# The output products of a pair-mixing kernel, taken image by image with a signal each

## The reference

```python
x = x + pair_mix(group_norm(x))     # layer 1
x = x + blur(group_norm(x))         # layer 2

# pair_mix, for v = group_norm(x) of shape (2, 64, 64, 64), last dimension D = 64
a = v @ Wa + ba
b = v @ Wb + bb
g = sigmoid(v @ Wg + bg)
ab = einsum('bijk,bikl->bijl', a, b)   # a 64x64 product per image and channel
return g * ab @ Wo + bo
```

## Time and profile before

| what | us |
|---|---|
| median of three runs | 68.85 |
| the runs | 68.38, 68.85, 69.01 |
| profiled execution, its time | 68.02 |
| profiled execution, its span | 66.2 |
| PE busy | 50.2 (76%) |
| DVE busy | 44.7 (67%) |
| POOL busy | 42.3 (64%) |
| ACT busy | 30.6 (46%) |

### The profile page before, as it was taken

How to read it: one execution, slowest core, us unless ns; L and a number is a source line. 1 busy time by engine, 2 the same in 40 slices (tenths; PEclk the granted TensorE clock), 3 DMA queues, 4 the chain that set the end, 5 groups by cost and what they waited for, 6 DMA issues and landing times.

```text
span 66.2 us, 2441 instructions
## 1 busy us (share of the span) xinstructions
PE 50.2 (76%) x1026; PEld 37.2 (56%) x1026; DVE 44.7 (67%) x123; ACT 30.6 (46%) x52; POOL 42.3 (64%) x52
## 2 busy tenths in 40 slices
PE   3999989876979979998629499867079659999100
PEld 3996967643749848676318178634069552464000
DVE  0092199989646598463999975499964399961750
ACT  5300012444554244956971963996621697423400
POOL 1000419469999999048999978486963719999300
PEclk9999999999999999999999999999995555558965
DMA  0799990000000000000000033100404000040074
GB/s 0 280 233 299 349 354 11 0 10 0 0 10 0 0 10 0 5 10 0 0 10 0 22 136 127 41 10 0 163 0 158 10 0 0 5 158 0 31 286 158
DMA packets 2603, 4.78 MB, mean 72 GB/s; under 512 B 288, under 2 KB 416, under 8 KB 2592
## 3 DMA queue, kind: packets, MB, share of 16 engines
q1 hardware_dynamic: 2592, 4.62, 19.7%
HBM read 2.52 MB, written 2.10 MB: 70 GB/s over the span
## 4 chain that ended last, share of the span: by engine, by line
PE 48%; DVE 26%; issue 6%; ACT 4%; DVEq 0%
PE ps_ag L665 10%; PE ps_ab L610 8%; PE ps_ot L650 7%; DVE x L441 5%; PE ps_ot L577 4%; PE ps_ab L634 4%; DVE zt L434 4%; DVE part L388 4%; PE ps_s L558 3%; DVE bsb L425 3%; PE ps_ag L598 3%; PE ps_ag L622 3%; DVE part L383 2%; PE ps_s L565 2%; ACT gate L305 2%
## 5 line engine op out<-in xcount | busy, mean ns | idle before, releaser
L242 POOL TENSOR_TENSOR y<-y,prod 128x512 f32<-128x512 f32 x12 | 16.5, 1379 | 3.8 <-DVE y L448 3.1
L208 POOL TENSOR_TENSOR rstd<-veps,half 128x2 f32<-128x2 f32 (+1 forms) x7 | 5.6, 802 | 12.6 <-DVE veps L418 12.4
L236 POOL TENSOR_TENSOR xb<-xs,par 128x512 f32<-128x512 f32 x8 | 10.5, 1338 | 1.5 <-issue 1.5
L327 ACT ACTIVATE prod<-x,coef 128x512 f32<-128x512 f32 x12 | 8.2, 712 | 4.4 <-POOL coef L219 4.4
L292 ACT ACTIVATE rt<-ps_ot 128x512 f32<-128x512 f32 x7 | 3.9, 595 | 11.3 <-PE ps_ot L577 11.3
L550 PE MATMUL ps_h<-zeros 128*128 128x128 f32 x46 | 8.2, 346 | 1.0 <-DVE zeros L457 1.0
L550 PEld LDWEIGHTS ps_h<-zeros 128*128 128x128 f32 x46 | 7.5, 252 | 1.0 <-DVE zeros L457 1.0
L448 DVE SCALAR_TENSOR_TENSOR y<-x,coef,y 128x512 f32<-128x512 f32 x6 | 6.7, 1118 | 1.9 <-POOL y L224 1.9
L298 ACT ACTIVATE at<-ps_ag,par 128x512 f32<-128x512 f32 x8 | 5.5, 687 | 5.0 <-PE ps_ag L598 4.8
L305 ACT ACTIVATE gate<-ps_ag,par 128x512 f32<-128x512 f32 x8 | 5.5, 682 | 4.1 <-PE ps_ag L622 4.1
L665 PE MATMUL ps_ag<-x,diag 128*128 128x512 f32 (+4 forms) x12 | 7.0, 719 | 0.0
(11 more groups left out here) (50 smaller groups left out, 80.4 us busy)
## 6 DMA issues: line engine op xcount, KB each, us to landing
xs<-x SPq DMA_DIRECT2D x8, 256.0 KB, 5.2
out<-y SPq DMA_DIRECT2D x8, 256.0 KB, 2.0
par<-params SPq DMA_DIRECT2D x1, 289.5 KB, 4.4
par<-params SPq DMA_DIRECT2D x1, 128.0 KB, 4.1
```

Of the source, the lines that this page charges most:

```text
L236: nc.gpsimd.tensor_tensor(xb[:, w, b, :, :], xs[:, w, b, :, :], bo.broadcast_to([128, ROWS, D]), ALU.add).then_inc(xb_ready, 1)
L242: return nc.gpsimd.tensor_tensor(y[:, w, b, :, :], y[:, w, b, :, :], prod[:, n % 2, k, :, :], ALU.add)
L327: nc.scalar.activation(prod[:, n % 2, k, :, :], x1[:, w, b, 1:ROWS + 1, k:D + k], ACT.Copy, scale=coef[:, w, b, k + 2:k + 3]).then_inc(pro ...
```

## The change

`product_o` goes over the images first: all sixteen products that write bank 0 of `ps_ot` (image 0), then the sixteen that write bank 1. `o_done` is raised at the end of each sixteen, so twice a wave, and each of the two x1_outs waits for its own signal. Which operands meet, and where each result lands, is the same as before.

```diff
             def x1_out(w, b):
-                if b == 0:
-                    dve.wait_ge(o_done, w + 1)
+                dve.wait_ge(o_done, 2 * w + b + 1)
                 dve.wait_ge(xb_ready, 2 * w + b + 1)
...
-                for r in range(ROWS):
-                    for h in range(2):
+                for b in range(2):
+                    for r in range(ROWS):
                         for t in range(2):
 
+                            h = b ^ t
                             last = nc.tensor.matmul(
-                                ps_ot[64 * t:64 * t + 64, h ^ t, 64 * r:64 * r + 64],
+                                ps_ot[64 * t:64 * t + 64, b, 64 * r:64 * r + 64],
                                 zt[64 * h:64 * h + 64, w, 128 * r + 64 * t:128 * r + 64 * t + 64],
                                 W_O[64 * h:64 * h + 64, :], start=True, stop=True)
-                last.then_inc(o_done, 1)
+                    last.then_inc(o_done, 1)
```

## The result

The changed kernel is slower: the ratio of its time to that of the kernel before is 1.0188 (95% interval 1.0153 to 1.0222) over 20 runs of each, about 1.3 us. The medians of all 20 are 69.53 and 69.07 us; they hold disturbed runs, which the ratio leaves out. The profiled execution took 69.10 us (68.02 before) with a span of 67.3 (66.2). Forecast were 70.6 us as the likeliest and 68.9 to 71.1 as the range.

What follows compares the result with a forecast made beforehand. The chain of waits was taken as the bound, through O at waves 0 and 3 only (TensorE busy 76%); 0.83 + 0.93 = 1.76 us on the 68.85 us median gave 70.6 us, range 68.9 to 71.1.

Steps and rivals of the forecast that it cites:

- Image 0's signal comes at the old end of the group: O group: image 0's sixteen products use two quadrants and need 16 rounds, as long as the whole group before.
- The even-pace rival: O group: two quadrants keep up, so the 0.61 us gain at wave 3 stands, 68.2 us; chance 0.07.
- Rounds of two last as long as rounds of four; k = 14: O group: a round starts two instructions, not four, in equal time; k, rounds added to the 16, taken as 14.
- Wave 0: +0.83 us: Wave 0's O at full clock: 14 x 0.059 us, all on the chain through product_g and the gate.
- Waves 1 and 2: nothing: O ends 0.83 us later but still before x1_out, which starts behind filter_right; zero cost.
- Wave 3: +0.93 us: Wave 3 at half clock: image 1's signal 1.54 us later, 0.61 us of it under the first x1_out.
- k from 9 to 16: The forecast's own span of added O rounds: 0.91 us (69.8) to 2.09 us (70.9), chance 0.58.
- the rival with k = 7: Case of far look-ahead (chance 0.27 for k 1 to 8): seven rounds added to O, 0.57 us, 69.4 us.
- The tail keeps its lengths: After wave 3's x1_outs: apart from their 0.9 us gap, the rest of the tail takes as long as before.
- Far look-ahead: O group: image 1 fills idle quadrants early, k = 1 to 8, 68.9 us at k = 1; chance 0.27.
- One bank at a time: O group: row halves take turns in one ps_ot bank, 64 rounds, k = 48, about 78 us; chance 0.03.
- The clock: Near 50 us: the fall comes ahead of a statistics product, doubling it and product_ab, 1.0 us on top; chance 0.05.

Runs made afterwards that it cites:

- blocks8: Kernel before with O's products in blocks of eight of one image, then eight of the other, one signal at the end; ratio 1.0152 to the kernel before.
- blocks4: Kernel before with O's products in blocks of four of one image, then four of the other, one signal at the end; ratio 0.9992 to the kernel before.
- waves12: Image order and two signals at waves 1 and 2 alone, old order at the others; ratio 0.9973 to the kernel before.
- wave3: Image order and two signals at wave 3 alone, old order elsewhere; ratio to the kernel before 1.0104, in the second series (_b) 1.0096.
- filter_between: Changed kernel with filter_right of wave 2, image 0, moved between wave 3's two x1_outs; ratio 1.0140 to the kernel before.
- order_only: Changed kernel without the signal in the middle: image order in all waves, one signal after the 32nd product; ratio 1.0317 to the kernel before.
- wave0: Image order and two signals at wave 0 alone, old order elsewhere; ratio to the kernel before 1.0109, in the second series (_b) 1.0212.
- rowhalves: Kernel before with wave 3 split by rows: rows 4 to 7 to ps_ab, signal after sixteen products, x1_outs by row halves; ratios 0.9896 and 1.0007.
- signals: Changed kernel with the old product order and its two waits, both released by the group's end; ratio 1.0032 to the kernel before.

## Why the prediction was right, step by step

- *Image 0's signal comes at the old end of the group.* Right: 1.19 and 2.03 us behind O's first product, 1.23 and 2.05 before. The even-pace rival is out.
- *Rounds of two last as long as rounds of four; k = 14.* Right, and 13 by the gate. The three products that the rows of before showed PE looking past are nearly all that there is; blocks8 and blocks4 confirm it at two more sizes.
- *Wave 0: +0.83 us.* +0.74, and all of it arrives, as said: from wave 0's O to wave 3's it is 29.98 us, before 29.22.
- *Waves 1 and 2: nothing.* Right, by waves12.
- *Wave 3: +0.93 us.* The term that was mis-sized: +0.64. Image 1's signal came 1.25 us behind image 0's, not 1.54. Some 13 rounds were left over and not 14, and a round at half clock is 0.107 us and not 0.11 (in the chain before, two instructions of 512 columns at L665 took 1.71 us); that is 1.39. Most of the rest is the way out of the last results, which ran at full clock again and took 0.22 us; where the whole of O was at half clock (wave3's first profile) it was 1.35. Of the 1.25 us 0.61 lie under the first x1_out, as said.
- *The sum: +1.76 us.* 1.38 by the two places, 1.3 by the ratio. The likeliest time was 1.1 us above the median: 0.4 to 0.5 from the sum, the rest from the base, 68.85 us, the median of three runs, when the lowest of the 20 were at 67.7 to 68.
- *The range.* 69.53 us lies in it, but below the 69.8 to 70.9 that k from 9 to 16 was to give, and next to the 69.4 of the rival with k = 7. That it lies in the range is owed to the room made for that rival; by the time alone the rival would have won. The ratio and the traces say k = 13.
- *The tail keeps its lengths.* Its length is the same, 10.75 us, but not its chain. The tail then hung on POOL behind `filter_right`, which filter_between shows; I had it on `halo` and the last products alone. Even before the change the way over POOL ended hardly earlier. ACT's x1b started at 60.72 us there; in the changed kernel VectorE follows 0.92 us behind it (62.75 - 61.83), which makes 61.64, and PE let VectorE go at 61.68. That explains why the length did not change when PE's clock did.
- *Far look-ahead* (k up to 8): out. The trace disagrees here with the Trainium skill's 64-deep reorder window ("TensorE: Matmul & The Clock Gate", Packing small matmuls, The mechanism), if that is taken for matmuls of other quadrants: 64 instructions, weight loads counted, stand in image 0's half, and image 1 did not start until 13 rounds were gone. With the same section's strict program order of starts it disagrees too: products of product_g start among O's.
- *One bank at a time*: out. Image 0's half has both row halves of the array writing into one bank, at full pace. *The clock*: it did not fall earlier; it came back sooner and fell once more.

## What to carry to other kernels

When small products share the array by quadrants, the order of the products is part of the tiling: each short run of neighbours has to touch all quadrants (here that also means both banks), and a signal "half-way" is only early if the first half uses all of them too. Before splitting a group for an earlier signal, ask which quadrants (and which banks) the first part can use; here the split by rows has all four, the split by images two. And look at what stands behind the wait that gets longer: a step that was ready (`filter_right`) may be the one that another engine hangs on.

## What the runs showed of the hardware

- PE starts products of different quadrants out of program order, but in this kernel only about three rounds ahead: 1, 7 and 13 rounds lost at full clock for blocks of 4, 8 and 16 products.
- The granted clock is not the same from run to run. In order_only's profile it fell for a while in the middle of the kernel as well, where PE waits 1.1 us for VectorE, as it does in the kernel before without a fall:

```profile
PEclk9999999999999999999965899999996589658965
...
34.51 0.49 PE L662 MATMUL ps_h<-x,par 128*128 128x128 f32 x2 [1.11 <-DVE x L441]
35.10 1.13 PE L610 MATMUL ps_ab<-par,rt 64*64 64x64 f32 x32
36.17 1.97 PE L577 MATMUL ps_ot<-par,gn 128*128 128x128 f32 x8
```

  product_b and the transposes took 1.13 and 1.97 us there; at full clock the transposes are 1.09. The profiles of wave0, wave0_b, wave3, rowhalves and signals have such a fall in the middle as well. Their spans, with order_only's, are 67.0 to 69.2 us, those of the profiles without it 66.0 to 67.3, so it is a likely part of the scatter between runs.
- The half-clock stretch that starts near 50 us differs too. With the image order at wave 3 (changed kernel, order_only, wave3, wave3_b, filter_between) it lasts 3.4 us, two or three of the page's slices; in the kernel before, in waves12 and in blocks8 it lasts some 10 us, in wave0 and wave0_b nearly 14, and in blocks4 and both rowhalves profiles about 7. In signals it is as short as in the changed kernel, with the old order. So the longer O can't be the only cause, and the cause is open. The tail gained nothing by the full clock: from the second x1_out to the end of the last instruction it takes 10.74 to 10.78 us in all profiles with `filter_right` behind the pair but wave0's, where half clock lasted to about 63 us and it took 10.91.
